# Last routed layer prepared group by group inside the attention before it, with fixed expert regions and the bias in a weight row

## What is computed

```python
x = x + tanh(g_xattn[3]) * attention(layernorm(x), ctx, ctx, mask, Wq, bq, Wk, bk, Wv, bv, Wo, bo)   # 16 heads of 8
x = x + tanh(g_ffn[3])   * moe(layernorm(x), gate_w, gate_b, w1, b1, w2, b2)

def moe(x):                       # D = 128, E = 8 experts, F = 512, TOP_K = 2
    logits = flat @ gate_w + gate_b
    topv, topi = top_k(logits, 2)
    routing = zeros.at[rows, topi].set(softmax(topv))
    for e in range(8):
        h = gelu(flat @ w1[e] + b1[e])
        acc += (h @ w2[e] + b2[e]) * routing[:, e]
```

## Time and profile before

| | |
|---|---|
| median of three runs | 2011.6 us |
| the profiled execution | 2011.66 us, span 2009.9 us |
| mean granted TensorE clock | 0.904 |
| attention of the last layer | about 1444 to 1712 us of the span |
| last feed-forward, preparation | 1712.4 to 1789.5 us |
| last feed-forward, 71 tiles | 1789.5 to 1982 us |
| last feed-forward, sum and store | 1982 us to the end |

### The profile page before, as it was taken

The page is one execution under the profiler, slowest core; times in us unless marked ns, Lnnn a source line. Parts: engine busy times, 40 slices in busy tenths (PEclk is TensorE's granted clock), DMA queues, the critical chain, the costliest instruction groups (busy, mean ns, idle before and its releaser), DMA issues. The chain is left out here.

```text
span 2009.9 us, 38821 instructions
## 1 busy us (share of the span) xinstructions
PE 1648.7 (82%) x12780; PEld 1233.6 (61%) x12796; DVE 1288.4 (64%) x3301; ACT 1212.7 (60%) x4200; POOL 734.5 (37%) x671
## 2 busy tenths in 40 slices
PE   4399997699999399989599657998399998569993
PEld 4355554499999166666599655455266666447883
DVE  5599998488888666666477564123357766664444
ACT  2199996399999187878377522433178887223333
POOL 2155554255555411111278510012210100256774
PEclk9699999799999699999799776998599999569997
DMA  4310001100000333332000202000234331301114
GB/s 132 100 64 1 1 1 33 43 1 1 1 2 1 84 95 81 92 79 54 25 1 0 85 2 89 1 0 1 73 80 99 99 88 38 134 23 48 50 53 143
DMA packets 49360, 100.39 MB, mean 50 GB/s; under 512 B 8747, under 2 KB 16221, under 8 KB 47445
## 3 DMA queue, kind: packets, MB, share of 16 engines
q1 hardware_dynamic: 43126, 86.09, 15.4%
q0 software_dynamic: 4608, 9.32, 1.6%
q10 hardware_dynamic: 1440, 2.62, 0.6%
HBM read 69.19 MB, written 28.77 MB: 49 GB/s over the span
## 5 line engine op out<-in xcount | busy, mean ns | idle before, releaser
L592 ACT ACTIVATE B_E<-B_logits,B_m 128x32 f32<-128x32 f32 (+1 forms) x1792 | 362.6, 371 | 9.4 <-DVE B_m L561 8.3
L1261 ACT ACTIVATE L_E<-L_sc,L_negm 128x128 f32<-128x128 f32 x1024 | 299.0, 402 | 112.4 <-DVE L_negm L1171 111.7
L598 POOL TENSOR_TENSOR B_E<-B_E,B_r 128x512 f32<-128x512 f32 x256 | 267.6, 1046 | 259.2 <-DVE B_r L580 259.2
L1171 DVE TENSOR_REDUCE L_negm<-L_sc 128x4 f32<-128x512 f32 x256 | 174.4, 684 | 112.3 <-PE L_sc L1334 104.4
L561 DVE TENSOR_REDUCE B_m<-B_logits 128x16 f32<-128x512 f32 (+1 forms) x256 | 172.6, 675 | 37.8 <-PE B_logits L552 30.7
L1332 PE MATMUL L_sc<-KS,L_QS 128*128 128x512 f32 x256 | 141.6, 554 | 66.2 <-DMA L_QS<-L_qsplit 55.3
L575 DVE TENSOR_REDUCE B_r<-B_E 128x16 f32<-128x512 f32 (+1 forms) x256 | 172.7, 675 | 2.4 <-POOL B_E L598 1.3
L1269 ACT ACTIVATE L_PT<-L_pt 128x512 f32<-128x512 f32 x256 | 166.0, 651 | 0.6 <-PE L_pt L1342 0.6
L1342 PE MATMUL L_pt<-ident,L_E 128*128 128x128 f32 x1024 | 156.9, 276 | 1.6 <-ACT L_PT L1269 1.6
L550 PE MATMUL B_logits<-B_phihi,B_xhi 128*128 128x512 f32 x256 | 153.8, 601 | 5.2 <-DVE B_philo L537 2.5
L1342 PEld LDWEIGHTS L_pt<-ident,L_E 128*128 128x128 f32 x1024 | 123.8, 142 | 24.0 <-ACT L_E L1261 2.0
(11 more groups left out here) (350 smaller groups left out, 3709.9 us busy)
## 6 DMA issues: line engine op xcount, KB each, us to landing
KS<-L_ksplit SPq DMA_DIRECT2D x192, 64.0 KB
L_QS<-L_qsplit SPq DMA_DIRECT2D x42, 256.0 KB, 4.0
F_w<-in_F_w SPq DMA_DIRECT2D x4, 2048.0 KB, 9.0
ew<-in_expert_w SPq DMA_DIRECT2D x1, 4096.0 KB, 15.5
L_cT<-in_ctxT SPq DMA_DIRECT2D x16, 256.0 KB, 4.7
L_ksplit<-L_khi SPq DMA_DIRECT2D x16, 256.0 KB, 2.0
L_ksplit<-L_klo SPq DMA_DIRECT2D x16, 256.0 KB, 2.3
L_qsplit<-L_qhi SPq DMA_DIRECT2D x14, 256.0 KB, 2.7
```

What stands on the lines that cost most here:

```text
L592: ins = nc.scalar.activation(e[:, cols], self.bank(k)[:, cols], ACT.Exp, bias=self.m[:, k % 4, g:g + 1])
L598: self.st.nc.gpsimd.tensor_tensor(e, e, self.r[:, k % 2, :].unsqueeze(2) .to_broadcast([128, self.ng, self.size]), ALU.mult).then_inc(self ...
L1171: nc.vector.tensor_reduce(negm[:, k % 4, :], sc[k % 2][:].rearrange("p (h k) -> p h k", h=NHG), AX.X, ALU.max, negate=True).then_inc(s["ma ...
L1261: ins = nc.scalar.activation(e[:, h * 128:(h + 1) * 128], sc[k % 2][:, h * 128:(h + 1) * 128], ACT.Exp, bias=negm[:, k % 4, h:h + 1])
```

## The change

- **Routing by group.** A new class `Route` keeps tables in SBUF. In the last layer's attention, group m of the feed-forward's rows is normalised at the end of group m+1, and transposed, given logits, top two, ranks and slots in group m+2, in units 1, 3, 4 to 10, 11 and 13 to 15. The last two groups (m = 6, 7) are done in the last stage.
- **Fixed regions.** Each expert has a region of 4096 rows in a DRAM table `route_rows`. A row's slot is the count so far plus its rank, so it can be written at once: GpSimd scatters the group with 8 indexed DMAs of 128 rows x 129 numbers (the 129th is the place of the result). The table is filled beforehand with neutral rows by 33 DRAM to DRAM transfers of 1024 rows, issued by SyncE in the feed-forward of the second layer.
- **Tiles at register rows.** A tile is 128 neighbouring rows, which SyncE loads at a row number held in a register. GpSimd has no gather left in the loop.
- **Bias in a weight row.** Normalised rows have mean zero, so feature 0 is minus the sum of the others. It is replaced by the constant 1, row 0 of `w1` is subtracted from rows 1 to 127, and row 0 becomes `b1`. The fourth matmul goes. The subtraction and the split of `w1` are done expert by expert on GpSimd in the attention: SyncE loads `wr` and `wb`, and stores the two parts to DRAM, from where the last stage loads them.
- The bounds check behind TensorE's value loads is left out.

The core of the diff:

```diff
+    def scatter(self, g, m):
+        ...
+        for c in range(TOPK):
+            for j in range(GB):
+                g.indirect_dma_start(self.xs_d, bass.IndirectOffsetOnAxis(self.slot[u][:, c, j:j + 1], 0),
+                                     self.XR[u][:, j, c, :], None).then_inc(self.scattered[u], 16)
+    def fill(self, sp, d):
+        ...
+        for e in range(NX):
+            for i in range(4):
+                at = e * self.R + i * 1024
+                sp.dma_start(self.xs_d[at:at + 1024, :], d["F3_fill"][e * 1024:(e + 1) * 1024, :]).then_inc(self.filled, 16)
...
+    ROUTE_PUT = {"rows": 1, "logits": 3, "ranks": 11} if route else {}
+    PICK, SLOT, NORMALISE = 4, 13, 15
...
+            def load_weights(e):
+                if e:
+                    sp.wait_ge(s["w_folded"], e)
+                sp.dma_start(wr[0:1, :], d["F3_b1_rows"][e:e + 1, :]).then_inc(s["wr_in"], 16)
+                sp.dma_start(wr[1:128, :], d["F3_w1"][1:128, e, :]).then_inc(s["wr_in"], 16)
+                sp.dma_start(wb[1:128, :], d["F3_w1"][0:1, e, :].to_broadcast([127, FF])).then_inc(s["wr_in"], 16)
+            def store_weights(e):
+                sp.wait_ge(s["w_parts"], 2 * (e + 1))
+                for i, part in enumerate((whi, wlo)):
+                    sp.dma_start(route.w1_d[i][:, e, :], part[:].bitcast(F32)).then_inc(route.w1_put, 16)
             for n in range(NG):
                 ...
                 spread(n)
                 if n + 2 < NG:
                     ...
                     load_ctx(n + 2)
+                if route:
+                    load_weights(n)
+                    if n:
+                        store_weights(n - 1)
...
+            def fold(e):
+                g.wait_ge(s["wr_in"], 48 * (e + 1))
+                if e:
+                    g.wait_ge(route.w1_put, 32 * e)
+                nc.gpsimd.tensor_tensor(wr[:], wr[:], wb[:], ALU.subtract).then_inc(s["w_diff"], 1)
+                ...
             for n in range(NG):
                 if n + 1 < NG:
                     split("k", n + 1)
                 if n + 1 < NG:
                     split("q", n + 1)
+                if route:
+                    fold(n)
                 if n:
                     tail.gpsimd(g, n - 1, (n - 1) % 2)
+                if route and n >= 2:
+                    route.scatter(g, n - 2)
+                if route and n:
+                    route.complete(g, n - 1)
...
 (last stage, SyncE)
+            sp.wait_ge(s["rtab_ready"], 1)
+            for u in range(2):
+                sp.wait_ge(route.scattered[u], 16 * route.PUTS * NG // 2)
+            for i in range(NT):
+                ...
+                sp.dma_start(xg[i % RG][:], route.xs_d[bass.ds(rows_at[i % PER], 128), :]).then_inc(xg_in[i % RG], 16)
...
-                nc.tensor.matmul(dst, xhi[u][:], lo, start=False, stop=False)
-                nc.tensor.matmul(dst, ones2[:], b1r[:, bass.ds(e, 1), :].rearrange("p a f -> p (a f)"),
-                                 start=False, stop=True).then_inc(s["h_ps"], 1)
+                nc.tensor.matmul(dst, xhi[u][:], lo, start=False, stop=True).then_inc(s["h_ps"], 1)
```

More of the change, by code:

```diff
@@ L37 @@
 NEG = -(2.0 ** 100)
+LOW = -3.0e38
 class Steps:
@@ L968, in stage_attn @@
                 turn_of["out", n - 1] = len(turn_of)
+            for use in ROUTE_PUT:
+                if n >= 2 and ROUTE_PUT[use] == w:
+                    turn_of[use, n - 2] = len(turn_of)
     turn_of["out", NG - 1] = len(turn_of)
@@ L1197, in add_constant, with route_part @@
                 return steps.mark(nc.vector.tensor_tensor(xg, xg, gcb[:].unsqueeze(1).to_broadcast([128, GB, D]), ALU.add))
+            route_mark = [0]
+            def route_part(m, w, half):
+                if not route or m < 0:
+                    return
+                if PICK <= w and 2 * (w - PICK) + half < route.PICKS:
+                    i = 2 * (w - PICK) + half
+                elif SLOT <= w and 2 * (w - SLOT) + half < route.PARTS - route.PICKS:
+                    i = route.PICKS + 2 * (w - SLOT) + half
+                else:
+                    return
+                a = turn_of["logits" if i < route.PICKS else "ranks", m]
+                if i in (0, route.PICKS):
+                    v.wait_ge(s["aux_full"], a + 1)
+                if route_mark[0]:
+                    steps.need(route_mark[0])
+                if i == route.PARTS - 1 and m >= 2:
+                    v.wait_ge(route.scattered[m % 2], 16 * route.PUTS * (m // 2))
+                route_mark[0] = steps.mark(route.choose(m, i, aux[a % 2]))
+                if i in (0, route.PICKS + 1):
+                    steps.need(route_mark[0])
+                    v.sem_inc(free(a), 1)
+                if i == route.PICKS - 1:
+                    steps.need(route_mark[0])
+                    v.sem_inc(route.M_ready, 1)
+                if i == route.PARTS - 1:
+                    steps.need(route_mark[0])
+                    v.sem_inc(route.slot_ready, 1)
             v.wait_ge(s["aux_full"], 1)
@@ L1286, in _ @@
                             upper(use, n + 1)
+                    if route and n >= 2 and w == ROUTE_PUT["rows"]:
+                        t = turn_of["rows", n - 2]
+                        a.wait_ge(s["aux_full"], t + 1)
+                        if n >= 3:
+                            a.wait_ge(s["aux_full"], turn_of["logits", n - 3] + 1)
+                        nc.scalar.activation(xrT[:], aux[t % 2][:], ACT.Copy).then_inc(free(t), 1)
             for k in range(NU - TURN, NU):
@@ L1325, in output, with put_route @@
                                            W["WoT"][:], start=True, stop=True)
+                ins.then_inc(s["aux_full"], 1)
+            def put_route(use, m):
+                a = turn_of[use, m]
+                bank = aux[a % 2]
+                if use == "rows":
+                    t.wait_ge(route.xr_ready, m + 1)
+                if use == "logits":
+                    x = turn_of["rows", m]
+                    t.wait_ge(free(x), x // 2 + 1)
+                if m == 0:
+                    t.wait_ge(route.const_done, 7)
+                need_bank(t, a)
+                if use == "rows":
+                    ins = route.turn(m, bank)
+                elif use == "logits":
+                    ins = route.logits(bank, xrT)
+                else:
+                    ins = route.ranks(t, m, bank)
                 ins.then_inc(s["aux_full"], 1)
@@ L1382, in _ @@
                         output(n - 1)
+                    for use in ROUTE_PUT:
+                        if n >= 2 and ROUTE_PUT[use] == w:
+                            put_route(use, n - 2)
             for k in range(NU, NU + ATTEND):
@@ L1845, in stage_l2_ffn @@
         hT = [st.sb(f"hT{i}", [128, GD]) for i in range(2 * FC)]
-        match = [st.sb(f"match{i}", [128, 2 * SL]) for i in range(2)]
-        WT = [st.sb(f"WT{i}", [128, 2 * SL]) for i in range(2)]
+        room = [x[:].rearrange("p b c w -> p (b c w)") for x in route.XR]
+        match = [x[:, 0:2 * SL] for x in room]
+        WT = [x[:, 2 * SL:4 * SL] for x in room]
         iota, upper = st.sb("iota", [128, 2 * SL]), st.sb("upper", [128, 128])
@@ L2175, in stage_l3_ffn @@
+        sidx = st.sb("sidx", [128, NT], U32)
+        xg = [st.sb(f"xg{i}", [128, route.W]) for i in range(RG)]
         xhi, xlo = ([st.sb(f"x{k}{u}", [128, 128], F32R) for u in range(2)] for k in ("hi", "lo"))
@@ new lines, in _ @@
+            banks = {m: (yb[m % 2], tb[m % 2]) for m in LAST}
+            mark = {}
+            for i in range(route.PICKS):
+                for m in LAST:
+                    if i == 0:
+                        v.wait_ge(s["logits"], m - LAST[0] + 1)
+                    else:
+                        steps.need(mark[m])
+                    mark[m] = steps.mark(route.choose(m, i, banks[m][0]))
+            for m in LAST:
+                steps.need(mark[m])
+                v.sem_inc(route.M_ready, 1)
@@ new lines, in _ @@
+            for m in LAST:
+                steps.need(mark[m])
+                v.sem_inc(route.slot_ready, 1)
+            v.wait_ge(s["c_in"], 16)
+            steps.link(nc.vector.tensor_tensor(cnt[:], route.base[0:1, :], route.ebase[0:1, :], ALU.subtract))
+            steps.link(nc.vector.tensor_tensor(cmp[:], cnt[:].unsqueeze(2).to_broadcast([1, NX, 32]),
+                                               steps128.unsqueeze(1).to_broadcast([1, NX, 32]), ALU.is_gt))
+            steps.link(nc.vector.tensor_reduce(tiles[:], cmp[:], AX.X, ALU.add))
@@ L2488, in _ @@
+            for m in LAST:
+                t.wait_ge(s["xT_done"], m - LAST[0] + 1)
+                route.logits(yb[m % 2], xT[m % 2]).then_inc(s["logits"], 1)
+            for m in LAST:
+                route.ranks(t, m, tb[m % 2]).then_inc(s["ranked"], 1)
             t.wait_ge(s["G_ready"], 1)
```

487 lines of the change are left out of this document (248 added, 239 removed).

## The result

Over 20 runs each the changed kernel took a median of 2029.1 us (2019.7 to 2040.0), the kernel before 2018.9 us (2000.7 to 2029.1): ratio 1.0068, 95% interval 1.0046 to 1.009. The change costs about 10 us. The forecast was 2062 us, 50 us over its base; the sign was right and the stated range (2015 to 2140) holds the time, but the loss is a fifth of the one forecast.

The account below looks back on a forecast made before the run. K's landing, behind one-engine weight loads, was taken to bound attention groups, TensorE the tile loop. 2011.7 - 16.3 - 8.5 (loop) - 36 (preparation) + 110 (attention) + 1 (end) = 2062 us; range 2015 to 2140.

Parts of the forecast that it names:

- What bounds the kernel: Attention: a transfer chain of 30.0 us a group; delaying K's landing by more than about a microsecond lengthens every group.
- The weight loads: Attention: 254 rows through one DMA engine at 0.096 us, 24.4 us; groups 46.1 instead of 30.4 us; six boundaries 94 us.
- the forecast's own formula: Whole kernel: 2062 + 7 x (L - 24.4) us, L being a group's weight loads in the attention; 2037 at 20.8, 2137 at 35.1.
- The 13.0: Attention: us from issuing `KS` to the next group's `QS`, while `KS` and written Q land; kept in the 46.1 us group.
- The rest of the attention: Attention without the slow loads: TensorE's 1.7 us a group and K written 1 to 3 us later, +11 us.
- The end: End of the program: one more barrier, about 1 us.
- Preparation: Before the last stage's tile loop: slots +12.7, last scatter issued by +33.9, first product +41 instead of 77.1; gain 36 us.
- Tile loop: Last stage's loop: -24.8 us, 16.3 from the dropped bias matmul over 71 tiles, 8.5 from the dropped check at nine loads.
- The fill: Second layer's feed-forward: 33 DRAM to DRAM transfers, 17.4 MB, 49 us, hidden.
- rival C: Fill not hidden: at 88 GB/s it takes 198 us, next context loads 40 us behind; 2102 or 2003 us; chance 0.05.
- A: Rival in the attention: 127-row loads spread over many engines, about 1.5 us, only +11 remains; kernel 1963 us; chance 0.14.
- B: Rival in the attention: one engine at 0.138 us a row, 35.1 us of loads; kernel 2137 us; 0.15 of main case's chance.

Follow-up runs that it names:

- 112 and 15: Changed kernel with each weight load of 127 partitions cut into transfers of 112 and 15 partitions: 1963.5 us, ratio 0.9757 to the kernel before; run again 1963.8 us.
- 122: Changed kernel with each load of 127 partitions cut into 122 and 5 partitions: 1965.3 us, ratio 0.977 to the kernel before.
- 124: Changed kernel with each load of 127 partitions cut into 124 and 3 partitions: 2014 us in one run, in a disturbed set.
- one of the forms: Changed kernel with loads cut into 112 and 15 partitions and GpSimd drains added: ratio 0.9883 to the kernel before in the disturbed set; again 1957.0 us, 0.9734.

## Why the prediction was wrong

**What bounds the kernel: right.** K's landing was named as what lengthens every group, and it does. The sum of one group in the changed trace, from the `QS` of group 1, is 5.6 (`QS` issued to first score) + 23.5 (to `KS`) + 11.6 (to the next `QS`) = 40.7 us; forecast 5.4 + 27.7 + 13.0 = 46.1.

**The weight loads: right mechanism, mis-sized term.** "I take 0.096, being loads alone, into 128 partitions: 254 x 0.096 = 24.4 us" is the step that failed. A row took 0.079 us, the loads 20.0 us. With them the six boundaries came to 63.3 us instead of 94. The price came from the read back, with a share of 0.76 of sixteen engines at work. That such a row's time holds the others' load too is argued, not shown, since the transfers differ as well; the numbers are: with `QS`, context and loads together a share of 0.99 moved 221 GB/s (the window at 1518 of 112 and 15), 0.147 us for 2048 bytes and one engine, while in the stores at 375 GB/s it was 0.087; a lone engine needs 0.079, and two or four nearly the same. The lower bound, 0.082 from rows 5, was the nearest row and still a little too high; the text had said that "an engine alone may be quicker than sixteen together" and used it only for the range. The Trainium skill, page "DMA: Bandwidth & Descriptors", section "Specifications", gives about 27 GiB/s an engine; the estimate from it was 17.9 us and 2017 us. Measured were 26 GB/s and 20.0 us. The page's figure was the nearer, 10% off to the other side.

In the forecast's own formula, 2062 + 7 x (L - 24.4), L = 20.0 gives 2031 us; the median was 2029. That nearness is in part chance. Averaged over the six groups, `QS` to `KS` took 29.7 us where the formula with L = 20.0 has 28.7, and `KS` to the next `QS` took 11.3 where it has 13.0. The 13.0 was one group's; the mean before was 12.4, and why it became 11.3 is open. So of the 5.1 us a group that the forecast was too high, the stretch with the loads has 3.4 and the one behind it 1.7. Other terms cancel too (below).

**The rest of the attention: about right, with a part that was missing.** The forecast without the loads was +11; the forms with 112 and 15 and no further change in the attention have +13.5 to +18.4 in five traces. In this are 4.0 us of GpSimd's drain, which no step had; the other 9.5 to 14.4 may hold the 1.7 us a group of TensorE's added work, but the run that doubled it could not show it. That part is argued, not shown. In the changed kernel the last group's +6.4 us (forecast +6, for GpSimd's waits) hold the same 4.0 of the drain, so that hit is in part luck.

**The end: a missing term.** "One more barrier at the end, about 1 us" was 4.5: 3.8 of it are again GpSimd's drain, 8.5 us instead of 4.7. The profile of before had the sign of it: a last drain of 4.65 us in the one stage with indirect DMAs, 1.1 us at the attention's end, and the change puts 48 indirect DMAs into the attention.

**Preparation: right.** Slots at +12.7 (measured 12.5), sixteen scatters as the longest piece with the last issued by +33.9 (ended at +33.0), first product at +41 (39.4). Gain 37.7 against 36.

**Tile loop: right.** The bias matmul 16.3 against 16.4 in its own run. The check 8.5 against 11.0: the step had taken it from TensorE's idle time alone. From tile to tile, a step across a value load with the check is 1.0 to 1.1 us longer than the others at four loads and 1.7 to 1.9 at the last four, 11.4 in all; without the check no step is longer there. Tile to tile 2.14 us, forecast 2.13. GpSimd's gather was worth nothing beyond, as said.

**The fill: hidden, as said**, shown by doubling it and by its 313 GB/s, where rival C needed less than about 110. Rival C falls.

**Rivals.** A (loads spread) was wrong for this kernel, and its number was right for a kernel in which they are: 1963 us forecast, 49 below its base; 1963.5 and 1963.8 measured with 112 and 15, 45 and 47 below the kernel before beside them. B (0.138 us a row) is refuted by 26 GB/s. Of what the text said it would see, groups 42 to 57 us apart and waits of 10 us and more for `QS` came out below (41.0; 6.2 to 9.1); K's landing 10 us after its write and the share of one sixteenth came out. A was said to decide from three engines on; two engines, 10 us, already fit into the gap.

**The balance.** Against the forecast of +50.2 for the changed stages stand +17.1: the attention 31.6 less, the loop 3.3 less, the preparation 1.7 less, the end 3.5 more. (A second trace of the changed kernel, the one of the table above, gives +15.6 instead of +17.1.) The forecast also stood on a base of 2011.7 us, 7 below the median of before over 20 runs.

## What to carry to other kernels

Before a load is cut to "all rows but the first", look at the number: SyncE's transfer over 127 partitions goes through one DMA engine, at 26 GB/s, and what the same queue issues next waits for that engine. The divisor rule that fits 127, 122 and 124 here says the same of any prime above 16, but only 127 was run. Two transfers of 112 and 15 partitions, or GpSimd's queue, took the loss away: an attention of 296.5 and 303.8 us instead of 361.1. And price a single engine from rows in which few engines work: here a row's time with all sixteen busy was up to 1.9 times that of a lone one. Where GpSimd has issued indirect DMAs, look at its drain at the next barrier, and put one where it has time.

## What the runs showed of the hardware

- The rate of a DMA engine hardly falls while few work: 26 GB/s for one, 51 to 54 for two, about 100 for four. Sixteen together moved 221 GB/s (loads mixed with `QS`) to 375 GB/s (while K and the weight parts were stored).
- SyncE can be held at an issue by rows that are still waiting: it stood 5.5 us at its issue of `wb` and 10.1 us at the next store while one engine worked through the rows, and at the first group 9.2 us; with 112 and 15 the two took 0.9 and 0.4 us. That a queue was full is inferred.
- GpSimd's drain lasts as long as the engine's own last operations still run, and 0.083 us more for each DMA that it has issued since the last drain. At the attention's end the operation left is 1.0 us: 1.1 us with no such DMA, 5.1 with 48, 7.1 with 48 and 24 plain ones. With one more transfer of 127 rows it is 7.1 us with 48, as 3.1 us of operations are left. At the end of the program 1.3 us are left: 1.4 us with none, 8.5 with 87. And an earlier stage without any has 7.9 us, with 7.8 us of operations left. The kernel before, with 142 since its last drain, took 4.65 us, which the same rule does not give; what bounds it there is open.
- In one set of runs two kernels' engines waited tens of us with nothing to wait for that the profile shows, in stretches of the attention; one of the forms ran again elsewhere and did not. Their attention took 345 and 351 us, where that form took 291 when it ran again, and only the rows of waits for issue showed the reason.
